# A selective-scan and expert-FFN kernel: the FFN's second layer one step later in TensorE's order

## Chip, cores and metric

One core of one Trainium2 chip. The metric is the time of one execution on the device, in microseconds (us). The kernel before took 3166.0 us (median of 3 runs, 3164.98 to 3170.4).

## What is computed

The input `x` has 32 rows (batch entries) of 512 tokens of 256 channels. Each row is normalised (`xn`), goes through a forward and a backward selective scan with 16 states each, and the sum is gated by an expert FFN. Cut to what matters:

```python
def _selective_scan(x, x_proj_w, dt_proj_w, dt_proj_b, A_log, Dp):
    A = -jnp.exp(A_log)
    dbc = jnp.einsum('bld,nd->bln', x, x_proj_w)
    delta, Bm, Cm = jnp.split(dbc, [DT_RANK, DT_RANK + D_STATE], axis=-1)
    delta = jax.nn.softplus(jnp.einsum('blr,dr->bld', delta, dt_proj_w) + dt_proj_b)
    deltaA = jnp.exp(delta[..., None] * A)
    BX = delta[..., None] * Bm[:, :, None, :] * x[..., None]
    ...
    y = jnp.einsum('blds,bls->bld', hs, Cm)
    return y + Dp * x

def _L0_ffn_ref(hidden_states, Wp1, bp1, Wp2, bp2, W1, b1, W2, b2, Wo, bo):
    ...
    h = jax.nn.gelu(jnp.einsum('bsh,bhf->bsf', hidden_states, w1) + b1[sel][:, None, :], approximate=False)
    reasoned = jnp.einsum('bsf,bfh->bsh', h, w2) + b2[sel][:, None, :]
    out = reasoned @ Wo + bo
    return hidden_states + 0.3 * out

xn = _layernorm(x, axis=-1)
s = scan_forward(xn) + scan_backward(xn)
g = _silu(_L0_ffn_ref(xn, ...))
x = x + s * g
```

The expert `sel` is picked once per row from its last token. The kernel multiplies W2 by Wo at the start, so that per row only two layers remain: `xn` by W1, then Gelu, then the product with W2·Wo.

## The kernel before, in words

The 32 rows are worked one after the other, each in 32 steps, one for each state (16 forward, 16 backward). All five engines have a program of their own, written out by hand; they meet by semaphores alone, and each engine works its own program strictly in its order. In step `s`:

- VectorE scans state `s` (`hs`, line 861) over 128 x 1024 values (two halves of the channels by 512 tokens), then multiplies the states of the step before by C (`hc`, line 840), for the states in `ON_DVE`. In step 1 it also forms the output `og` of the row before (line 833), and in step 0 the mean and variance of a later row (line 811).
- ScalarE makes the decay of state `s + 2` (line 692), scales `dxb` (line 595) for the states in `TURNED`, and copies what TensorE leaves in the one PSUM bank `front` (`fps`).
- GpSimd multiplies by B (`bx`, line 481) for the states that are not in `TURNED`, and by C (`hc`, line 469) for those in `POOL_C`, which are 2, 4, 5, 7, 9 and so on.
- TensorE broadcasts C of state `s + 1` into the PSUM bank `c` (line 1076), turns `dxb` of state `s + 3` into PSUM for the scan (line 1068), adds the skip term (line 1083) and the state products into `y` (line 1093). The broadcast waits until VectorE has used the last one.

While row `r` is scanned, the front of row `r + 1` (transposes, projections, step sizes, FFN) is worked in the same steps, in small pieces. The tables at lines 37 to 46 say in which step each piece is issued, separately for TensorE, ScalarE and GpSimd; numbers of 32 and more mean a step of the row's own scan (35 is its step 3). All pieces share the bank `front`, so each piece of TensorE waits until ScalarE has copied the one before.

The second FFN layer is issued by `ffn_out` (line 1024). It has eight parts, and two of them make one quarter, which is the gate's input for 128 tokens: four f32 products of `hT` with `w2o_sb` (line 1036), a bias product (line 1038) and the addition of `xn` (line 1039). Quarters 1 and 2 fill the bank, ScalarE's first gate copy (`gate_input`, line 637) moves it into `zz`, quarters 3 and 4 fill it again, and the second gate copy moves that. `FFN_OUT` lists the steps of the eight parts and `GATE` those of ScalarE's two copies; row 0 has tables of its own, `FFN_OUT_FIRST` and `GATE_FIRST`. The quarters wait for the Gelu (line 641), which ScalarE does at the end of step 31, between two loads of its function table. Later in ScalarE's order come the normalised row `xn` (line 558), its transposed copies (line 566) and the copy `projected` (line 575), for which VectorE's `low` (line 819) waits.

Within a step the order on TensorE is: broadcast, turn, skip term, adds, then the pieces of the front:

```python
if s + 1 in ON_DVE:
    broadcast_c(row, par, s + 1)
...
if s in ON_DVE:
    add_state(row, s)
front(row, par, s + STEPS, last)
if not last:
    front(row + 1, 1 - par, s)
```

Of the kernel before, what the change touches and what calls it, by code (L numbers as in the profile page):

```python
# [5 lines left out]
def mamba_moe_block(nc, x, xw_f, dtw_f, dtb_f, alog_f, d_f, xw_b, dtw_b, dtb_b, alog_b, d_b,  # L6
# [35 lines left out]
    LOG1P, STEPSIZE, DX, CUT = (26, 36), (27, 39), (28, 43), (29, 44)  # L42
    DX_TURN, DX_COPY = (28, 29, 44, 45), (30, 31, 46, 47)
    FFN_IN, HIDDEN, GELU = (16, 16, 18, 18, 20, 20, 22, 22), (18, 20, 22, 24), 31
    FFN_OUT, GATE = (31, 31, 32, 32, 34, 34, 35, 35), (35, 38)
    FFN_OUT_FIRST, GATE_FIRST = (33, 33, 34, 34, 36, 36, 37, 37), (36, 38)
    Y_OUT, Y_RESIDUAL = 1, 4
    SKIP = {0: ((0, 0), (2, 0)), 1: ((0, 1), (1, 0), (1, 1), (2, 1)), 4: ((3, 0), (3, 1))}
# [1196 lines left out]
```

## Time and profile before

| | |
|---|---|
| median of 3 runs | 3166.0 us |
| the profiled execution | 3168.72 us |
| its span in the profile | 3166.9 us |
| mean granted TensorE clock | 0.942 of full speed |
| busy: VectorE / ScalarE / GpSimd / TensorE | 96% / 94% / 93% / 82% |

The profile calls TensorE's matrix products PE and its weight loads PEld, VectorE DVE, ScalarE ACT, GpSimd POOL. Times are from the start of the span. In a timeline, consecutive like instructions are merged into one line with their count, and the bracket gives the idle time ahead of the line and what ended it; the end of a line overlaps the start of the next a little, since engines are pipelined. One row of the input takes some 96 us.

### The profile page before, as it was taken

How to read it: one execution, taken by the hardware profiler on the slowest of the kernel's cores; microseconds unless marked ns; L12 is line 12 of the kernel's file. 1: busy time of each engine (PE TensorE's matmuls, PEld its weight loads, DVE VectorE, ACT ScalarE, POOL GpSimd, SP SyncE). 2: the span in 40 equal slices, each digit the busy share in tenths (PEclk: the TensorE clock that was granted, in tenths of full speed). 3: DMA queues.
4: the chain of work that ended last, by engine and by line, in shares of the span. 5: the costliest groups of instructions: out<-in, count | busy, mean ns of one | idle time of the engine just before them, and what ended most of it. 6: DMA issues, size and time to landing. Idle time of an engine off the chain costs nothing. (4 is left out here: it accounts for less than half of the span.)

```text
span 3166.9 us, 49729 instructions
## 1 busy us (share of the span) xinstructions
PE 2591.2 (82%) x16278; PEld 2075.5 (66%) x16278; DVE 3027.4 (96%) x1964; ACT 2971.9 (94%) x5306; POOL 2945.8 (93%) x1454
## 2 busy tenths in 40 slices
PE   7888878888878888788888788887788887888886
PEld 5666666666667666666666666666666665666665
DVE  3999999999999999999999999999999999999998
ACT  5999999999999999999999999999999999999995
POOL 2899999999999999999999999999999999999996
PEclk9999999999999999999999999999999999999998
DMA  5443334443344443344433344433344333444331
GB/s 171 148 129 112 115 117 129 135 127 109 116 127 123 135 120 115 106 131 136 128 109 112 123 125 139 124 111 113 125 129 134 118 114 108 130 136 127 104 113 50
DMA packets 268759, 385.83 MB, mean 122 GB/s; under 512 B 44491, under 2 KB 118996, under 8 KB 268500
## 3 DMA queue, kind: packets, MB, share of 16 engines
q1 hardware_dynamic: 268500, 382.64, 39.8%
q8 instruction: 130, 2.13, 0.3%
q14 instruction: 129, 1.06, 0.1%
HBM read 340.59 MB, written 25.18 MB: 115 GB/s over the span
## 5 line engine op out<-in xcount | busy, mean ns | idle before, releaser
L481 POOL TENSOR_TENSOR bx<-dx,b_sb 128x1024 f32<-128x1024 f32 x576 | 1364.4, 2383 | 48.3 <-DVE hs L861 46.3
L861 DVE TENSOR_TENSOR_SCAN hs<-decay,bx 128x1024 f32<-128x1024 f32 x576 | 1306.6, 2278 | 11.3 <-ACT decay L692 6.4
L1093 PE MATMUL y<-ident,hc 128*128 128x128 f32 x8192 | 1097.9, 283 | 35.9 <-DVE hc L840 35.9
L469 POOL TENSOR_TENSOR hc<-hs,c_sb 128x1024 f32<-128x1024 f32 x448 | 1057.1, 2369 | 52.6 <-DVE hs L861 51.7
L1093 PEld LDWEIGHTS y<-ident,hc 128*128 128x128 f32 x8192 | 970.1, 146 | 144.3 <-DVE hc L840 99.9
L861 DVE TENSOR_TENSOR_SCAN hs<-decay_sb,decay 128x1024 f32<-128x1024 f32 x448 | 1009.8, 2271 | 39.5 <-PE decay L1068 24.3
L692 ACT ACTIVATE decay<-delta,rate 128x512 f32<-128x512 f32 x1152 | 745.6, 684 | 38.8 <-DVE hs L861 38.2
L595 ACT ACTIVATE dxb<-dxT,btok 128x256 f32<-128x256 f32 x1792 | 762.6, 504 | 0.6 <-PE decay L1068 0.6
L840 DVE TENSOR_TENSOR hc<-hs,c 128x1024 f32<-128x1024 f32 x576 | 690.8, 1199 | 28.9 <-PE c L1076 20.5
L1068 PE MATMUL decay<-ident,dxb 128*128 128x128 f32 x3584 | 482.1, 281 | 150.0 <-DVE hs L861 120.8
L1068 PEld LDWEIGHTS decay<-ident,dxb 128*128 128x128 f32 x3584 | 414.0, 144 | 289.7 <-issue 217.1
L692 ACT ACTIVATE decay_sb<-delta,rate 128x512 f32<-128x512 f32 x896 | 589.2, 716 | 0.0
L1076 PE MATMUL c<-dbc,selector 128*128 128x512 f32 x576 | 292.7, 508 | 290.8 <-DVE hc L840 290.8
L1076 PEld LDWEIGHTS c<-dbc,selector 128*128 128x128 f32 x576 | 113.1, 196 | 353.4 <-DVE hc L840 348.8
L1036 PE MATMUL front<-w2o_sb,hT 128*128 128x256 f32 x1024 | 296.2, 441 | 31.3 <-issue 31.3
L1020 PE MATMUL front<-xnT,w_sb 128*128 128x512 f32 x512 | 244.2, 599 | 41.9 <-ACT delta L608 41.9
L1036 PEld LDWEIGHTS front<-w2o_sb,hT 128*128 128x128 f32 x1024 | 217.8, 224 | 73.3 <-issue 41.7
L456 POOL TENSOR_TENSOR lg<-lg,ex 128x1024 f32<-128x1024 f32 x64 | 151.3, 2364 | 35.8 <-ACT lg L625 34.8
L1020 PEld LDWEIGHTS front<-xnT,w_sb 128*128 128x128 f32 x512 | 87.4, 190 | 116.7 <-issue 61.2
L461 POOL TENSOR_TENSOR delta<-lg,delta 128x1024 f32<-128x1024 f32 x64 | 152.5, 2382 | 0.1
L446 POOL TENSOR_TENSOR dx<-delta,xnT 128x1024 f32<-128x1024 f32 x64 | 152.5, 2382 | 0.1
L488 POOL TENSOR_TENSOR og<-og,xres 128x1024 f32<-128x1024 f32 x32 | 75.5, 2361 | 61.3 <-DVE og L833 61.3
(128 smaller groups left out, 2190.1 us busy)
## 6 DMA issues: line engine op xcount, KB each, us to landing
b_sb<-b_scratch SPq DMA_DIRECT2D x576, 256.0 KB, 3.3
c_sb<-b_scratch SPq DMA_DIRECT2D x448, 256.0 KB, 3.6
xin<-in_L_attn_x_dram SPq DMA_DIRECT2D x32, 512.0 KB, 7.7
w_sb<-in_L_ffn_W_dram SPq DMA_DIRECT2D x32, 512.0 KB, 3.4
w2o_sb<-w2o_scratch SPq DMA_DIRECT2D x32, 512.0 KB
xres<-in_L_attn_x_dram SPq DMA_DIRECT2D x32, 512.0 KB, 5.3
out_dram<-og SPq DMA_DIRECT2D x32, 512.0 KB, 4.4
dbc<-high SPq DMA_DIRECT2D x64, 128.0 KB, 2.4
```

Source lines behind the costliest of these rows:

```text
L446: nc.gpsimd.tensor_tensor(dx[:, g, :, :], delta[:, g * (1 + par), :, :], xnT[:, par, :, :], ALU.mult).then_inc(s_dx, 1)
L469: nc.gpsimd.tensor_tensor(hc[:, s % RING, :, :], hs[:, s % HSLOTS, :, :], c_sb[:, i % CRING, :].unsqueeze(1).broadcast_to([P, DT, T]), ALU ...
L481: nc.gpsimd.tensor_tensor(bx[:, i % RING, :, :], dx[:, g, :, :], b_sb[:, i % BRING, :].unsqueeze(1).broadcast_to([P, DT, T]), ALU.mult).th ...
L595: A(dxb[:, (row * NT + i) % XSLOTS, c, :], dxT[:, g, c, :], ACT.Copy, scale=btok[:, par, c, g, n:n + 1]).then_inc(s_dxb, 1)
L692: return A(to[:, k, :], delta[:, g * (1 + par), k, :], ACT.Exp, scale=rate[:, g, k, n:n + 1])
L840: V.tensor_tensor(hc[:, s % RING, :, :], hs[:, s % HSLOTS, :, :], cps[:, :].unsqueeze(1).broadcast_to([P, DT, T]), ALU.mult).then_inc(s_hc, 1)
L861: V.tensor_tensor_scan(hs[:, s % HSLOTS, :, :].rearrange("p k t -> p (k t)")[:, u], factor.rearrange("p k t -> p (k t)")[:, u], data.rearr ...
L1020: ins = M(fps[:, :], w1_sb[:, k, j * P:(j + 1) * P], xnT[:, par, k, :], start=(k == 0), stop=(k == DT - 1))
L1036: M(to, hT[:, j, c * P:(c + 1) * P], w2o_sb[:, j, :], start=(j == 0), stop=False)
L1068: ins = nc.tensor.transpose(dps[s % DSLOTS][:, k, c * P:(c + 1) * P], dxb[:, (row * NT + i) % XSLOTS, c, k * P:(k + 1) * P], ident[:, :])
L1076: M(cps[:, :], selector[:, N + n:N + n + 1].broadcast_to([P, P]), dbc[:, par, g, :], start=True, stop=True).then_inc(s_cps, 1)
L1093: ins = M(yps[:, c, k * P:(k + 1) * P], hc[:, s % RING, k, c * P:(c + 1) * P], ident[:, :], start=False, stop=(s == ADDED[-1]), is_transpo ...
```

## The change

The first two quarters are issued one step later each (31 and 32 become 32 and 33), the last two as well (34 and 35 become 35 and 36), and ScalarE's first gate copy moves from step 35 to 36. The second gate copy stays at 38, and row 0's own tables stay.

```diff
-    FFN_OUT, GATE = (31, 31, 32, 32, 34, 34, 35, 35), (35, 38)
+    FFN_OUT, GATE = (32, 32, 33, 33, 35, 35, 36, 36), (36, 38)
     FFN_OUT_FIRST, GATE_FIRST = (33, 33, 34, 34, 36, 36, 37, 37), (36, 38)
```

TensorE around the border of two rows, from the broadcast of C for state 0 to that for state 3. In `c<-dbc,selector`, `c` is the result and the rest the inputs. Before:

```order
L1076 MATMUL c<-dbc,selector 128x512
L1093 MATMUL y<-ident,hc 128x128 x8
L1036 MATMUL front<-w2o_sb,hT 128x256 x4
L1038 MATMUL front<-bias,ones 128x256
L1039 MATMUL front<-xn,ident 128x256
L1076 MATMUL c<-dbc,selector 128x512
L1083 MATMUL y<-dskip_diag,xnT 128x128 x2
L1093 MATMUL y<-ident,hc 128x128 x8
L1036 MATMUL front<-w2o_sb,hT 128x256 x4
L1038 MATMUL front<-bias,ones 128x256
L1039 MATMUL front<-xn,ident 128x256
L1083 MATMUL y<-dskip_diag,xnT 128x128 x4
```

With the change:

```order
L1093 MATMUL y<-ident,hc 128x128 x8
L1076 MATMUL c<-dbc,selector 128x512
L1083 MATMUL y<-dskip_diag,xnT 128x128 x2
L1093 MATMUL y<-ident,hc 128x128 x8
L1036 MATMUL front<-w2o_sb,hT 128x256 x4
L1038 MATMUL front<-bias,ones 128x256
L1039 MATMUL front<-xn,ident 128x256
L1083 MATMUL y<-dskip_diag,xnT 128x128 x4
L1093 MATMUL y<-ident,hc 128x128 x8
L1036 MATMUL front<-w2o_sb,hT 128x256 x4
L1038 MATMUL front<-bias,ones 128x256
L1039 MATMUL front<-xn,ident 128x256
```

The first quarter has moved from ahead of the broadcast for state 1 to behind the add of state 0; the second, from ahead of the skip term of step 1 to behind that step's add.

TensorE from the broadcast for state 3 to that for state 6. Before:

```order
L1076 MATMUL c<-dbc,selector 128x512
L1068 MATMUL decay<-ident,dxb 128x128 x8
L1036 MATMUL front<-w2o_sb,hT 128x256 x4
L1038 MATMUL front<-bias,ones 128x256
L1039 MATMUL front<-xn,ident 128x256
L1068 MATMUL decay<-ident,dxb 128x128 x8
L1093 MATMUL y<-ident,hc 128x128 x8
L1036 MATMUL front<-w2o_sb,hT 128x256 x4
L1038 MATMUL front<-bias,ones 128x256
L1039 MATMUL front<-xn,ident 128x256
L1083 MATMUL y<-dskip_diag,xnT 128x128 x2
L1093 MATMUL y<-ident,hc 128x128 x8
```

With the change:

```order
L1076 MATMUL c<-dbc,selector 128x512
L1068 MATMUL decay<-ident,dxb 128x128 x16
L1093 MATMUL y<-ident,hc 128x128 x8
L1036 MATMUL front<-w2o_sb,hT 128x256 x4
L1038 MATMUL front<-bias,ones 128x256
L1039 MATMUL front<-xn,ident 128x256
L1083 MATMUL y<-dskip_diag,xnT 128x128 x2
L1093 MATMUL y<-ident,hc 128x128 x8
L1036 MATMUL front<-w2o_sb,hT 128x256 x4
L1038 MATMUL front<-bias,ones 128x256
L1039 MATMUL front<-xn,ident 128x256
L1076 MATMUL c<-dbc,selector 128x512
```

The two turns for states 5 and 6 now stand side by side; the same instructions as before stand between the two broadcasts.

ScalarE at its first gate copy. Before:

```order
L692 ACTIVATE decay<-delta,rate 128x512 x2
L595 ACTIVATE dxb<-dxT,btok 128x256 x4
L637 ACTIVATE zz<-front 128x512
L595 ACTIVATE dxb<-dxT,btok 128x256 x4
L692 ACTIVATE decay_sb<-delta,rate 128x512 x2
```

With the change:

```order
L692 ACTIVATE decay<-delta,rate 128x512 x2
L595 ACTIVATE dxb<-dxT,btok 128x256 x8
L637 ACTIVATE zz<-front 128x512
L692 ACTIVATE decay_sb<-delta,rate 128x512 x2
L595 ACTIVATE dxb<-dxT,btok 128x256 x4
```

The copy `zz` stands one block of `dxb` later. VectorE's and GpSimd's orders do not change.

## Rows read from the trace of the kernel before

**Rows 1.** The page, busy us (share of the span) and instructions

```profile
PE 2591.2 (82%) x16278; PEld 2075.5 (66%) x16278; DVE 3027.4 (96%) x1964; ACT 2971.9 (94%) x5306; POOL 2945.8 (93%) x1454
```

**Rows 2.** The page's costliest groups: count | busy, mean ns | idle before, releaser

```profile
L861 DVE TENSOR_TENSOR_SCAN hs<-decay_sb,decay 128x1024 f32<-128x1024 f32 x448 | 1009.8, 2271 | 39.5 <-PE decay L1068 24.3
...
L840 DVE TENSOR_TENSOR hc<-hs,c 128x1024 f32<-128x1024 f32 x576 | 690.8, 1199 | 28.9 <-PE c L1076 20.5
```

**Rows 3.** Line 833's instructions: ns min/median/max, first and last start

```profile
L833 DVE TENSOR_TENSOR og<-y,zz x32: 1195/1199/1224, 179.7 to 3159.9; 128x1024 f32<-128x1024 f32 x32
```

**Rows 4.** VectorE's timeline at one row: start, us, engine, line [idle before]

```profile
1240.24 1.21 DVE L840 TENSOR_TENSOR hc<-hs,c 128x1024 f32<-128x1024 f32 x1
...
1243.57 1.20 DVE L840 TENSOR_TENSOR hc<-hs,c 128x1024 f32<-128x1024 f32 x1
...
1249.17 1.22 DVE L840 TENSOR_TENSOR hc<-hs,c 128x1024 f32<-128x1024 f32 x1
...
1253.43 2.29 DVE L861 TENSOR_TENSOR_SCAN hs<-decay_sb,decay 128x1024 f32<-128x1024 f32 x1 [0.84 <-PE decay L1068]
...
1258.48 1.22 DVE L840 TENSOR_TENSOR hc<-hs,c 128x1024 f32<-128x1024 f32 x1 [0.58 <-PE c L1076]
...
1271.66 0.67 DVE L819 TENSOR_TENSOR low<-front,high 128x512 fp32r<-128x512 f32 x1
```

**Rows 5.** TensorE's timeline at the same row

```profile
1235.25 0.79 PE L1076 MATMUL c<-dbc,selector 128*128 128x512 f32 x1 [1.94 <-DVE hc L840]
1235.84 1.91 PE L1093 MATMUL y<-ident,hc 128*128 128x128 f32 x8
1238.38 3.75 PE L1036 MATMUL front<-w2o_sb,hT 128*128 128x256 f32 x8 [0.63 <-issue]
...
1242.62 0.58 PE L1076 MATMUL c<-dbc,selector 128*128 128x512 f32 x1
...
1244.35 1.89 PE L1036 MATMUL front<-w2o_sb,hT 128*128 128x256 f32 x8
...
1246.92 1.05 PE L1083 MATMUL y<-dskip_diag,xnT 128*128 128x128 f32 x8
...
1248.60 0.48 PE L1076 MATMUL c<-dbc,selector 128*128 128x512 f32 x1
...
1257.91 0.48 PE L1076 MATMUL c<-dbc,selector 128*128 128x512 f32 x1
```

**Rows 6.** Windows: length, PE, PEld, DVE, ACT, POOL busy, granted clock, DMA

```profile
1242.00:1258.00 16.00, 16.00 (x104) 13.64 (x103) 15.03 (x8) 15.32 (x37) 14.67 (x11) 1.00 0.31 99
1235.20:1242.00 6.80, 6.12 (x17) 4.45 (x17) 6.66 (x12) 6.76 (x7) 5.30 (x3) 0.50 0.37 131
```

**Rows 7.** ScalarE's timeline at the same row

```profile
1247.28 0.58 ACT L637 ACTIVATE zz<-front 128x512 f32<-128x512 f32 x1
1247.76 1.70 ACT L595 ACTIVATE dxb<-dxT,btok 128x256 f32<-128x256 f32 x4
...
1256.88 0.60 ACT L637 ACTIVATE zz<-front 128x512 f32<-128x512 f32 x1 [0.55 <-PE front L1039]
1257.57 2.08 ACT L558 ACTIVATE xn<-xin,shift,rs 128x256 f32<-128x256 f32 x4
1259.55 1.32 ACT L692 ACTIVATE decay_sb<-delta,rate 128x512 f32<-128x512 f32 x2
...
1270.80 0.58 ACT L575 ACTIVATE projected<-front 128x512 f32<-128x512 f32 x1
```

**Rows 8.** TensorE's timeline: the start of work at another stretch of low clock

```profile
1504.23 0.50 PE L1076 MATMUL c<-dbc,selector 128*128 128x512 f32 x1 [2.81 <-DVE hc L840]
```

**Rows 9.** Windows of these two stretches, columns as in rows 6

```profile
1504.80:1508.20 3.40, 3.40 (x18) 3.30 (x17) 3.40 (x3) 2.95 (x5) 3.34 (x3) 0.51 0.00 0
...
1526.08:1532.10 6.02, 6.02 (x15) 4.33 (x16) 5.55 (x5) 5.98 (x14) 3.56 (x3) 0.50 0.19 66
```

**Rows 10.** Grouped lines: line 637

```profile
L637 ACT ACTIVATE zz<-front 128x512 f32<-128x512 f32 x64 | 37.9, 592 | 26.8 <-PE front L1039 26.5
```

## The prediction

> **What bounds the kernel now.** The page's busy shares come first [rows 1]. VectorE is busy 96% of the span, GpSimd 93%, ScalarE 94%, TensorE 82%. VectorE runs the scans; a time can change only by changing how long VectorE is idle. Outside the head of the program its idle time is small: the costliest groups [rows 2] put 39.5 us before the scans of turned states and 28.9 us before its `hc` products, 68.4 us together. So little can a change of order give back, while nothing caps a loss.
>
> The period of a row comes from the `og` products, of which there are 32, the first at 179.7 and the last at 3159.9 us [rows 3]: 2980.2 / 31 = 96.14 us. I read one row in detail, the one whose `og` starts at 1239.13 (the next one comes 96.09 us later by the same count of work, close to the mean).
>
> VectorE's timeline there [rows 4] has two waits, both on TensorE: 0.84 us before scan 6, and 0.58 us before the product of state 6, which needs that state's C broadcast. TensorE's timeline [rows 5] says why. It waits 0.63 us for the Gelu, then runs from 1238.38 without a gap. The windows [rows 6] confirm it: busy 16.00 of 16.00 us from 1242.00 to 1258.00. So **TensorE, idle on average, is the late engine in the first seven steps of a row**, and the four quarters of the second FFN layer stand inside that stretch. It is a queue worked in order: what is put into it delays all behind it.
>
> **The change, part by part.** I call the quarters F01, F23, F45, F67, the broadcasts c0, c1, c3, c6 by their state, and T5, T6 the turns of b*x.
>
> Nothing is added or removed. F01 leaves the end of step 31, where it stood between c0's add and c1, and goes behind c1, the skip term and the add of state 0. The others move down likewise; F67 still stands ahead of c6. The move is made for rows 1 to 31, 31 times. No DMA and no GpSimd instruction moves, and SyncE's waits for these units are due at its step 10, long after.
>
> 1. *The place that F01 leaves.* TensorE's last add before it starts at 1235.84 and takes 1.91, to 1237.75. Now the next instruction is c1, which waits for VectorE's product of state 0: 1240.24 + 1.21 = 1241.45, so it starts at about 1241.5. Before, c1 started at 1242.62. It is **1.12 us earlier**, but VectorE has no use for it: its product of state 1 comes at 1243.57 and did not wait [rows 4, 5]. TensorE idles 3.75 us instead of 0.63. The wait for the Gelu disappears, for F01 could start by 1238.38 as before.
>
> 2. *The place where F01 arrives.* At full clock a quarter takes 1246.92 - 1244.35 = **2.57 us** [rows 5]. From c1 to c3 stood c1, skip, add, F23, skip, add: 1248.60 - 1242.62 = 5.98 us, of which all now stays, plus F01. So c3 starts at 1241.5 + 5.98 + 2.57 = 1250.05, not 1248.60, if the clock is full.
>
> 3. *The clock.* TensorE ran at 1.2 GHz (granted 0.50) from 1235.2 to 1242.0 and at 2.4 GHz behind that [rows 6]. The low stretch began after 1.94 us without work, and ended after 3.6 us of unbroken work (1238.38 to 1242.0). At the row of 1526 it ended after 6.0 us of unbroken work (1526.08 to 1532.1), at 1504 after 4.0 (1504.23 to 1508.2) [rows 8, 9]. Now there is more idle time in the low stretch, and work begins at 1241.5; no row has that long a pause there. The bounds: nothing (the clock rises at 1242.0 anyway), and 6.0 us at half speed, 3.0 us lost. I take 4 us, as two of the three cases have, so **2.0 us lost**. That puts c3 at 1252.05.
>
> The Trainium skill, "TensorE: Matmul & The Clock Gate", Part 1, says that for modeling the ramp penalty is under 1% of a typical kernel span. By that rule this term would be at most 31.7 us in all, against my 31 x 2.0 = 62 us; the trace already has low stretches in every row looked at, so I keep the rows' figure.
>
> 4. *From c3 to c6.* The same instructions as before, in another order: 1257.91 - 1248.60 = 9.31 us. They ran without a gap before, so c6 starts at 1252.05 + 9.31 = 1261.36. That is 2.57 - 1.12 + 2.0 = **3.45 us later** per row. Inside it the shares differ. VectorE waits for c3 about 3.4 us (product 3 starts near 1252.6 instead of 1249.17). T6 now follows T5 directly, so the 0.84 us before scan 6 goes. At product 6 it waits again, some 1.6 us. Sum 5.0 against 1.42 before. F45 waits for ScalarE's first gate copy, which comes right behind F23 and takes 0.58 us [rows 7]; T5, T6 and an add (3 x 0.87 us) cover that, so it costs nothing.
>
> 5. *ScalarE behind it.* Its first gate copy stands one block of `dxb` later (4 copies, 1.70 us with the overlap), which alone is free. But it then waits for F23, until 1252.1; it would be there at 1248.9. The second copy waits for F67, until 1261.4, where it ran at 1256.88. ScalarE is thus 4.5 us late when VectorE is 3.45 late, about 1.1 us more. Behind the copy stand `xn` (2.0 us) and the decay of state 9 (1.3): 1261.4 + 0.7 + 2.0 + 1.3 = 1265.4. Scan 9 follows product 6 (1258.48, 1.2 us) and scan 8 (2.3 us [rows 2]), so it started near 1262.0 and would now at 1265.4, with nothing in hand. The late copy is also ahead of the copy `projected`, which ended at 1271.38, 0.28 us before VectorE's `low` [rows 7, 4]. So ScalarE's lag costs between 0 (it catches up, being idle 6% of the span [rows 1]) and 1.1 us; I take **0.8**, since 1.1 - 0.28 is what the second of these places shows.
>
> *The sum:* 3.45 + 0.8 = 4.25 us a row, times 31 = 131.8 us. The profiled execution took 3168.7 us (span 3166.9); 3168.7 + 131.8 = 3300.5. It stands 2.7 above the median of 3166.0, so the forecast is **3298 us**, 4.2% slower.
>
> **The rivals.** A measurement of this kernel can tell about 0.2%, 6 us, from no change.
>
> *The clock rises with the work* (term 3 near nothing, as the skill's rule would have it nearer than mine). Then c6 is 2.57 - 1.12 = 1.45 us late and ScalarE adds 0 to 0.8: 45 to 70 us, 3211 to 3236. For it: the rise at 1242.0 came in spite of a pause. Against: before that rise TensorE had worked, and now it has not.
>
> *The low clock lasts 6 us of work.* Term 3 is 3.0 and ScalarE's lag costs its 1.1: (1.45 + 3.0 + 1.1) x 31 = 172, so 3338. The row at 1526 speaks for it; others for less.
>
> *Faster: TensorE catches up.* T6 and c6 come in time, since F45 no longer stands between T5 and T6, and their waits of 0.84 us or more vanish: 31 x 0.84 = 26 us, 3140. It needs c3 out by 1249.17 - 0.55 = 1248.6, which leaves 7.1 us from 1241.5 for work that takes 5.98 + 2.57 = 8.55 at full clock. Only quarters under 1.1 us each would decide so; the rows have 2.57.
>
> *No change:* VectorE has 1.4 us of waits there that could absorb as much. But c6 itself is among the late ones, so there is no slack behind it; and the order shows that the move is made.
>
> **How the numbers follow.** Forecast 0.74, clock rises at once 0.10, long low clock 0.11, faster 0.03, no change 0.02. The range reaches from the upper part of the first rival, 3225, to the end of the second, 3338. Faster 0.03, within 0.2% 0.02, slower 0.95.
>
> **What would show it.** VectorE's wait before product 1 stays near nothing, one of 2.5 to 4 us appears before product 3, the one before scan 6 goes, and the one before product 6 grows to 1 to 2 us. TensorE shows a pause of 3 to 4 us ahead of c1 in each row, `<- DVE hc`, and the low stretch there is longer than 6.8 us. ScalarE's idle time before line 637, 26.8 us now [rows 10], passes 100 us. If the idle time before scans of line 861 grows by more than that of line 840, I am wrong about the place; if low stretches are not longer, about term 3.

## The result, and the profile after

The changed kernel takes 3301.3 us (median of 4 runs, 3300.4 to 3301.7) against 3165.5 us before: a ratio of 1.0426, with a 95% interval of 1.0408 to 1.0444. It is slower by 136 us. The profiled execution has a span of 3299.3 us.

The first rows to read are the same groups as in [rows 2], and line 637 as in [rows 10]:

```profile
L861 DVE TENSOR_TENSOR_SCAN hs<-decay,bx 128x1024 f32<-128x1024 f32 x576 | 1308.2, 2281 | 12.7 <-ACT decay L692 6.4
...
L861 DVE TENSOR_TENSOR_SCAN hs<-decay_sb,decay 128x1024 f32<-128x1024 f32 x448 | 1009.7, 2271 | 34.3 <-ACT decay_sb L692 17.7
L840 DVE TENSOR_TENSOR hc<-hs,c 128x1024 f32<-128x1024 f32 x576 | 690.9, 1199 | 149.0 <-issue 103.8
...
L637 ACT ACTIVATE zz<-front 128x512 f32<-128x512 f32 x64 | 38.5, 601 | 163.4 <-PE front L1039 163.4
```

The work of VectorE's groups is unchanged to 0.2%. Its idle time before its `hc` products grew by 120.1 us (28.9 to 149.0), while that before the turned scans fell by 5.2 and its releaser changed from TensorE's turns to ScalarE's decays. ScalarE waits six times as long for the quarters (26.8 to 163.4).

The period of a row, from line 833 as in [rows 3]:

```profile
L833 DVE TENSOR_TENSOR og<-y,zz x32: 1196/1201/1226, 178.6 to 3292.2; 128x1024 f32<-128x1024 f32 x32
```

(3292.2 - 178.6) / 31 = 100.44 us, 4.30 us more than the 96.14 before; 31 x 4.30 = 133 us, nearly all of the loss. One row in VectorE's timeline, from its `og` on, the places of [rows 4], and with them three waits that the kernel before had smaller or not at all:

```profile
1185.49 1.20 DVE L833 TENSOR_TENSOR og<-y,zz 128x1024 f32<-128x1024 f32 x1
...
1199.48 1.22 DVE L840 TENSOR_TENSOR hc<-hs,c 128x1024 f32<-128x1024 f32 x1 [3.97 <-issue]
...
1208.78 1.22 DVE L840 TENSOR_TENSOR hc<-hs,c 128x1024 f32<-128x1024 f32 x1 [1.39 <-PE c L1076]
...
1212.58 2.29 DVE L861 TENSOR_TENSOR_SCAN hs<-decay_sb,decay 128x1024 f32<-128x1024 f32 x1 [0.38 <-issue]
...
1222.92 0.69 DVE L819 TENSOR_TENSOR low<-front,high 128x512 fp32r<-128x512 f32 x1 [0.25 <-ACT projected L575]
1224.20 2.29 DVE L861 TENSOR_TENSOR_SCAN hs<-decay_sb,decay 128x1024 f32<-128x1024 f32 x1 [0.59 <-ACT decay_sb L692]
```

These are the products of states 3 and 6, scan 9, and the low part with the scan behind it. The wait before scan 6 is gone. In the kernel before, the scan behind the low part was this:

```profile
1272.70 4.46 DVE L861 TENSOR_TENSOR_SCAN hs<-decay_sb,decay 128x1024 f32<-128x1024 f32 x2 [0.36 <-issue]
```

From start to start the row divides into three stretches. From `og` to product 3 it takes 13.99 us, against 1249.17 - 1239.13 = 10.04 in the row of [rows 4]. From product 3 to product 6 it takes 9.30, against 9.31. From product 6 to the scan behind the low part it takes 15.42, against 14.22. So 1.20 us are lost behind product 6, more than the 0.86 by which the waits in brackets grew there (0.38 + 0.25 + 0.59 - 0.36): the rest stands in no bracket. Three instructions of this stretch that used to start some 0.1 us before the end of the one ahead no longer do. TensorE's timeline, with the C broadcasts for states 0, 1, 3 and 6 as in [rows 5]:

```profile
1181.61 0.50 PE L1076 MATMUL c<-dbc,selector 128*128 128x512 f32 x1 [1.94 <-DVE hc L840]
...
1187.87 0.80 PE L1076 MATMUL c<-dbc,selector 128*128 128x512 f32 x1 [4.88 <-DVE hc L840]
...
1191.02 2.96 PE L1036 MATMUL front<-w2o_sb,hT 128*128 128x256 f32 x8
...
1198.80 0.58 PE L1076 MATMUL c<-dbc,selector 128*128 128x512 f32 x1
...
1208.11 0.58 PE L1076 MATMUL c<-dbc,selector 128*128 128x512 f32 x1
```

From c1 to c3 it takes 10.93 us, from c3 to c6 9.31, the latter to the digit what it took before. At full clock the first stretch would take 5.98 + 2.57 = 8.55 by the rows of before, so low clock cost this row 2.38 us. In the next row the two broadcasts stand at 1289.13 and 1298.93, 9.80 apart, and it cost 1.25. The windows of both rows, columns as in [rows 6]:

```profile
1183.00:1193.20 10.20, 5.33 (x19) 4.79 (x20) 10.18 (x10) 10.14 (x20) 7.46 (x6) 0.50 0.18 55
1193.20:1208.00 14.80, 14.80 (x92) 12.26 (x91) 10.20 (x6) 9.59 (x21) 12.28 (x8) 1.00 0.33 107
1285.40:1292.20 6.80, 3.07 (x13) 2.98 (x14) 6.80 (x5) 6.74 (x16) 4.33 (x3) 0.50 0.21 74
```

The granted clock is at its lower level (1.2 GHz) for 10.2 us in one row and 6.8 us in the other, and rows of the two kinds follow each other almost to the end, 101.3 and 100.1 us long. ScalarE's two gate copies and what stands behind, as in [rows 7]:

```profile
1199.19 0.60 ACT L637 ACTIVATE zz<-front 128x512 f32<-128x512 f32 x1 [3.86 <-PE front L1039]
...
1208.49 0.60 ACT L637 ACTIVATE zz<-front 128x512 f32<-128x512 f32 x1 [1.84 <-PE front L1039]
1209.19 2.08 ACT L558 ACTIVATE xn<-xin,shift,rs 128x256 f32<-128x256 f32 x4
1211.17 1.32 ACT L692 ACTIVATE decay_sb<-delta,rate 128x512 f32<-128x512 f32 x2
```

The decay of state 9 ends at 1212.49, and scan 9 starts at 1212.58, having waited 0.38.

### The profile page after: what moved, and what is told of

Its sections match the earlier page's. It is cut to its first block and busy times, and to the rows that moved or that the text cites. A ratio compares the mean times of both kernels' runs of the same rounds, so it can differ in the third digit from the quotient of the medians.

```text
span 3299.3 us, 49729 instructions
## 1 busy us (share of the span) xinstructions
PE 2581.2 (78%) x16278; PEld 2092.4 (63%) x16278; DVE 3037.4 (92%) x1964; ACT 2970.1 (90%) x5306; POOL 2951.4 (89%) x1454
## 5 line engine op out<-in xcount | busy, mean ns | idle before, releaser
L1093 PEld LDWEIGHTS y<-ident,hc 128*128 128x128 f32 x8192 | 987.4, 147 | 139.7 <-DVE hc L840 94.5
L840 DVE TENSOR_TENSOR hc<-hs,c 128x1024 f32<-128x1024 f32 x576 | 690.9, 1199 | 149.0 <-issue 103.8
L1076 PE MATMUL c<-dbc,selector 128*128 128x512 f32 x576 | 301.2, 523 | 438.0 <-DVE hc L840 438.0
L1068 PE MATMUL decay<-ident,dxb 128*128 128x128 f32 x3584 | 497.9, 288 | 147.3 <-DVE hs L861 140.4
L1068 PEld LDWEIGHTS decay<-ident,dxb 128*128 128x128 f32 x3584 | 432.9, 149 | 280.3 <-issue 211.8
L1036 PE MATMUL front<-w2o_sb,hT 128*128 128x256 f32 x1024 | 258.4, 398 | 0.0
L1036 PEld LDWEIGHTS front<-w2o_sb,hT 128*128 128x128 f32 x1024 | 198.4, 204 | 24.6
L637 ACT ACTIVATE zz<-front 128x512 f32<-128x512 f32 x64 | 38.5, 601 | 163.4 <-PE front L1039 163.4
```

Of the source, the lines that this page charges most:

```text
L840: V.tensor_tensor(hc[:, s % RING, :, :], hs[:, s % HSLOTS, :, :], cps[:, :].unsqueeze(1).broadcast_to([P, DT, T]), ALU.mult).then_inc(s_hc, 1)
L1036: M(to, hT[:, j, c * P:(c + 1) * P], w2o_sb[:, j, :], start=(j == 0), stop=False)
L1068: ins = nc.tensor.transpose(dps[s % DSLOTS][:, k, c * P:(c + 1) * P], dxb[:, (row * NT + i) % XSLOTS, c, k * P:(k + 1) * P], ident[:, :])
L1076: M(cps[:, :], selector[:, N + n:N + n + 1].broadcast_to([P, P]), dbc[:, par, g, :], start=True, stop=True).then_inc(s_cps, 1)
L1093: ins = M(yps[:, c, k * P:(k + 1) * P], hc[:, s % RING, k, c * P:(c + 1) * P], ident[:, :], start=False, stop=(s == ADDED[-1]), is_transpo ...
```

## The experiments

Eleven kernels ran. All edits are against the changed kernel unless said otherwise; each time is set against the kernel before, run on the same chip.

### Which part of the move: TensorE's or ScalarE's

```diff
-    FFN_OUT, GATE = (32, 32, 33, 33, 35, 35, 36, 36), (36, 38)
+    FFN_OUT, GATE = (32, 32, 33, 33, 35, 35, 36, 36), (35, 38)
```

> TensorE's four quarters stand one step later as in the change, ScalarE's first gate copy stays at step 35. Theory (TensorE's order is the cause, the copy waits for the second quarter wherever it stands): 3295 to 3305 us, the same as the whole change. Rival (the copy's later place costs its block of dxb, 1.6 us a row): 31 x 1.6 = 50 us less, about 3250.

Measured: 3303.6 us, ratio 1.0437 (1.0419 to 1.0454). The whole loss is there without ScalarE's edit, but not by the same waits. With the copy one block of `dxb` earlier, product 6 does not wait; the scan ahead of it waits instead, for ScalarE's decay:

```profile
1203.91 2.29 DVE L861 TENSOR_TENSOR_SCAN hs<-decay,bx 128x1024 f32<-128x1024 f32 x1 [1.63 <-issue]
```

From product 3 to the scan behind the low part it takes 24.72 us in both kernels (1196.69 to 1221.41 here, 1199.48 to 1224.20 in the change). The second half alone, on the tables of before:

```diff
-    FFN_OUT, GATE = (31, 31, 32, 32, 34, 34, 35, 35), (35, 38)
+    FFN_OUT, GATE = (31, 31, 32, 32, 34, 34, 35, 35), (36, 38)
```

> The quarters stand as before, only ScalarE's first gate copy is one step later. Theory: the third quarter starts at 1249.79 in the row read, the copy would end at about 1249.5, so only rows with a longer low clock pay: 0 to 0.6 us a row, 3166 to 3184 us. Rival (the copy's place is worth 1.6 us a row): about 3215.

Measured: 3169.5 us, ratio 1.0015 (1.0006 to 1.0025). The later place of the copy costs 4 to 5 us by itself, and nothing where the copy waits for its quarter anyway.

### Which quarter

```diff
-    FFN_OUT, GATE = (32, 32, 33, 33, 35, 35, 36, 36), (36, 38)
+    FFN_OUT, GATE = (32, 32, 32, 32, 34, 34, 35, 35), (35, 38)
```

> Only the first quarter moves, from the end of step 31 to the end of step 0, directly ahead of the second. Theory: it carries the 3.45 us a row (place and clock), but the second quarter now ends 1.8 us sooner than with the whole change and the fourth 1.2 us sooner, so ScalarE is hardly late: 3166 + 107 = 3273, between 3250 and 3285. Rival (the loss is all TensorE's late C broadcasts and needs no ScalarE): 3301, as the whole change.

Measured: 3250.3 us, ratio 1.0263 (1.0246 to 1.0281), 84 us over the kernel before and at the lower edge of what was expected. VectorE's waits in one row:

```profile
1181.14 1.22 DVE L840 TENSOR_TENSOR hc<-hs,c 128x1024 f32<-128x1024 f32 x1 [2.93 <-issue]
...
1185.40 2.29 DVE L861 TENSOR_TENSOR_SCAN hs<-decay_sb,decay 128x1024 f32<-128x1024 f32 x1 [0.84 <-PE decay L1068]
...
1190.45 1.22 DVE L840 TENSOR_TENSOR hc<-hs,c 128x1024 f32<-128x1024 f32 x1 [0.58 <-PE c L1076]
...
1204.66 4.47 DVE L861 TENSOR_TENSOR_SCAN hs<-decay_sb,decay 128x1024 f32<-128x1024 f32 x2 [0.36 <-issue]
```

The three later waits are those of the kernel before, to the digit. One new wait, 2.93 us at product 3, is all that was added. Scan 9 and the low part do not wait for ScalarE: the second and fourth quarter end early enough here.

The complement:

```diff
-    FFN_OUT, GATE = (32, 32, 33, 33, 35, 35, 36, 36), (36, 38)
+    FFN_OUT, GATE = (31, 31, 33, 33, 35, 35, 36, 36), (36, 38)
```

> The first quarter stays in step 31; quarters two to four and the gate copy move as in the change. Theory: the broadcasts for states 3 and 6 keep their place behind the same work, but the quarters end 1.8 and 1.2 us later for ScalarE, which passes part of it on: 0.5 to 1.2 us a row, 3180 to 3203. Rival (only the first quarter matters): 3166, within 6.

Measured: 3211.7 us, ratio 1.0143 (1.0126 to 1.0160), 46 us over, a little above what was expected. VectorE's waits in one row:

```profile
1175.22 1.22 DVE L840 TENSOR_TENSOR hc<-hs,c 128x1024 f32<-128x1024 f32 x1 [1.27 <-PE c L1076]
...
1179.01 2.29 DVE L861 TENSOR_TENSOR_SCAN hs<-decay_sb,decay 128x1024 f32<-128x1024 f32 x1 [0.37 <-issue]
...
1189.33 0.69 DVE L819 TENSOR_TENSOR low<-front,high 128x512 fp32r<-128x512 f32 x1 [0.25 <-ACT projected L575]
1190.62 4.46 DVE L861 TENSOR_TENSOR_SCAN hs<-decay_sb,decay 128x1024 f32<-128x1024 f32 x2 [0.59 <-ACT decay_sb L692]
```

Here the product of state 6 waits 1.27 us instead of 0.58 after 0.84, so TensorE's part is the same as before; what is new are ScalarE's three waits, with 0.37 + 0.25 + (0.59 - 0.36) = 0.85 us in brackets, and 1175.22 to 1190.62, 15.40 us from start to start, as in the whole change (before: 14.22). The row shown takes 97.1 us, 1.0 more than the row of [rows 4]. It is the shortest of three kinds; the others take 98.0 and 98.4. In them TensorE's clock is still low when c1 is issued (to 1063.0, with c1 at 1061.5), and products 1 and 3 wait up to 0.47 and 0.59 us. The two halves of the move together make 84 + 46 = 130 us of the 136.

### The clock

The changed kernel, with transposes of the identity into the bank `front` in the pause that the first quarter left. They read nothing that the kernel makes, and the first quarter overwrites them.

```diff
+            def keep_busy(row, n):
+
+                pe.wait_ge(s_dxT, row * 4 + 2)
+                for i in range(n):
+                    nc.tensor.transpose(fps[:, i % C * P:(i % C + 1) * P], ident[:, :], ident[:, :])
...
                     if s in ON_DVE:
                         add_state(row, s)
+                    if s + 1 == STEPS and not last:
+                        keep_busy(row + 1, 28)
                     front(row, par, s + STEPS, last)
```

> The changed kernel with 28 more transposes of the identity into the free bank front in the pause that the first quarter left (their result is overwritten by the first quarter; 28 x 0.11 = 3.1 us of work at full clock in a pause of 3.7). Theory (term 3: low clock behind the pause costs about 2.0 us a row): 31 x 2.0 = 62 us less, 3225 to 3250. Rival (the order alone makes the loss, the clock nothing): 3301. If the filler itself delays the broadcast for state 1, above 3301.

Measured: 3243.4 us, ratio 1.0248 (1.0231 to 1.0265): 58 us less than the change, 1.9 a row. VectorE's waits in one row, and TensorE's filler, C broadcast for state 3 and clock:

```profile
1166.23 1.20 DVE L833 TENSOR_TENSOR og<-y,zz 128x1024 f32<-128x1024 f32 x1
...
1177.65 1.22 DVE L840 TENSOR_TENSOR hc<-hs,c 128x1024 f32<-128x1024 f32 x1 [1.41 <-issue]
...
1186.96 1.22 DVE L840 TENSOR_TENSOR hc<-hs,c 128x1024 f32<-128x1024 f32 x1 [1.38 <-PE c L1076]
...
1190.75 2.29 DVE L861 TENSOR_TENSOR_SCAN hs<-decay_sb,decay 128x1024 f32<-128x1024 f32 x1 [0.38 <-issue]
```

```profile
1164.03 4.41 PE L1204 MATMUL front<-ident 128*128 128x128 f32 x28
1168.61 0.50 PE L1076 MATMUL c<-dbc,selector 128*128 128x512 f32 x1 [0.16 <-DVE hc L840]
...
1176.98 0.58 PE L1076 MATMUL c<-dbc,selector 128*128 128x512 f32 x1
```

```profile
1162.00:1166.20 4.20, 3.85 (x20) 3.78 (x21) 4.05 (x10) 4.15 (x4) 4.03 (x2) 0.63 0.58 163
1166.20:1180.00 13.80, 13.64 (x95) 11.95 (x94) 12.39 (x9) 12.47 (x30) 11.19 (x9) 0.99 0.27 81
```

The low clock now falls on the filler and is over before c1 is issued. The wait at product 3 is 1.41 instead of 2.85 or 3.97; the others stay as they were. The clock is thus worth 1.44 to 2.56 us in a row, 2.0 in the mean. From c1 to c3 it takes 8.37 us at full clock, a little less than the 8.55 worked out above. Product 3 starts 11.42 us after `og`, 1.38 later than in the row of [rows 4]: that is what the place costs there, clock apart. Not every row is mended: in the row where c1 stands at 478 most of the filler ran at the lower clock and took 5.13 us, c1 came 0.9 us late, and product 3 waited 2.31.

### Are the late C broadcasts the cause, or only where it shows

```diff
-                    if s + 1 in ON_DVE:
+                    if s + 1 in ON_DVE and s + 1 not in EARLY_C:
                         broadcast_c(row, par, s + 1)
...
                     if s in ON_DVE:
                         add_state(row, s)
+                        for n in EARLY_C:
+                            if on_dve(n) == on_dve(s) + 1:
+                                broadcast_c(row, par, n)
```

with `EARLY_C = (3, 6)`.

> The changed kernel, but TensorE broadcasts C for states 3 and 6 right behind the add of states 1 and 3, ahead of the second and the fourth quarter, so that VectorE's products 3 and 6 need not wait for them. By step 4 of the prediction taken literally (the lateness of the broadcasts is the loss): the waits of 2.9 to 4.0 and 1.4 us a row go, down to 3301 - 31 x 4.8 = 3152. Rival (all of TensorE's unbroken work is late, the turns for states 5, 8 and 9 and ScalarE's gate copies with it, and the broadcast is only where it shows): the waits move to scans 5 and 9, 3290 to 3310 us.

Measured: 3317.6 us, ratio 1.0479 (1.0462 to 1.0497), 16 us more than the change and above both expectations. The waits of one row:

```profile
1201.68 1.22 DVE L840 TENSOR_TENSOR hc<-hs,c 128x1024 f32<-128x1024 f32 x1 [1.50 <-issue]
1205.06 4.46 DVE L861 TENSOR_TENSOR_SCAN hs<-decay_sb,decay 128x1024 f32<-128x1024 f32 x2 [2.16 <-PE decay L1068]
1210.11 2.29 DVE L861 TENSOR_TENSOR_SCAN hs<-decay,bx 128x1024 f32<-128x1024 f32 x1 [0.58 <-issue]
...
1214.37 2.29 DVE L861 TENSOR_TENSOR_SCAN hs<-decay_sb,decay 128x1024 f32<-128x1024 f32 x1 [0.86 <-PE decay L1068]
1217.58 2.29 DVE L861 TENSOR_TENSOR_SCAN hs<-decay_sb,decay 128x1024 f32<-128x1024 f32 x1 [0.92 <-ACT decay_sb L692]
```

Product 6 does not wait any more, product 3 waits less, and the sum is not smaller: scans 5 and 8 wait for TensorE's turns in its place, and scan 9 for ScalarE longer than before (0.92 against 0.38), since the broadcasts now stand ahead of the quarters. From product 3 to the scan behind the low part it takes 1201.68 to 1229.20, 27.52 us, against 24.72 in the change. In other rows product 3 waits only 0.24 or 0.67, and they take 101.5 and 100.7 us, little less than the 101.6 of the one shown; in the first of them a low clock further on in the row makes a scan wait 1.11 us for its turn, so part of the 16 us is the clock's. The broadcast is where the lateness shows. The cause is the length of TensorE's unbroken work from c1 on, whatever stands first in it.

### ScalarE's share

The decay of state 9 is made at the start of ScalarE's step 6, ahead of the second gate copy, instead of behind it and `xn`.

```diff
-    AHEAD, AHEAD_NEXT = {5: 8, 14: 22, 15: 24, 16: 26, 23: 28, 26: 29, 27: 30}, {29: 5}
+    AHEAD, AHEAD_NEXT = {5: 8, 6: 9, 14: 22, 15: 24, 16: 26, 23: 28, 26: 29, 27: 30}, {29: 5}
```

> The changed kernel, with ScalarE's decay of state 9 made at the start of step 6, ahead of the second gate copy, in whose wait it fits (1.2 us). Theory (term 5: ScalarE is late behind the gate copies): VectorE's wait of 0.37 us before scan 9 goes, and the ones at the low part (0.25 + 0.23 us more) shrink as ScalarE uses its idle time: 3262 to 3290 us. Rival (ScalarE's lag is hidden): 3301.

Measured: 3250.0 us, ratio 1.0265 (1.0248 to 1.0282): 51 us less than the change, more than expected. The profiled execution is the slowest of its four (3257.6). In its row at 1188 the waits are 2.92 at product 3, 1.39 at product 6 and 0.59 at the scan behind the low part; those before scan 9 and before the low part are gone. ScalarE at the second gate copy:

```profile
1195.13 1.32 ACT L692 ACTIVATE decay_sb<-delta,rate 128x512 f32<-128x512 f32 x2
1197.07 0.60 ACT L637 ACTIVATE zz<-front 128x512 f32<-128x512 f32 x1 [0.62 <-PE front L1039]
```

The decay fits in the wait, which shrank from 1.84 to 0.62 us. The direct gain is the 1.20 us between product 6 and the scan behind the low part (most rows are back at 14.2), 37 us in all. The other 14 us came from elsewhere: the wait at product 3 falls from 4.29 us in the first row to 3.0 in the fifth and is 2.8 to 2.9 in most behind, where the change has 2.85 and 3.97 in turn. A row of 98.9 us instead of 100.4 meets the low clock in another way. That is read from the trace and was not tested by itself.

### Both mends at once

The changed kernel with the filler of 28 and the earlier decay:

```diff
-    AHEAD, AHEAD_NEXT = {5: 8, 14: 22, 15: 24, 16: 26, 23: 28, 26: 29, 27: 30}, {29: 5}
+    AHEAD, AHEAD_NEXT = {5: 8, 6: 9, 14: 22, 15: 24, 16: 26, 23: 28, 26: 29, 27: 30}, {29: 5}
...
                     if s in ON_DVE:
                         add_state(row, s)
+                    if s + 1 == STEPS and not last:
+                        keep_busy(row + 1, 28)
```

> The changed kernel with both mends: 28 filler transposes and the decay of state 9 ahead of the gate copy. If the loss is place + clock + ScalarE, the two mends add up: 3301 - 58 - 51 = 3192, and what is left over 3165 is the place, 31 x (2.57 - 1.12) = 45 us at most: 3185 to 3212. Rival (the two mends cure the same wait): about 3240.

Measured: 3214.5 us, ratio 1.0156 (1.0141 to 1.0172), 2.5 us above the range expected, and 87 us less than the change instead of 109. What the second mend had won through the clock cannot be won twice; without it the sum is 58 + 37 = 95, and 8 us stay open. One row, and line 833, from the fastest of the four runs (3208.2):

```profile
1358.94 1.22 DVE L840 TENSOR_TENSOR hc<-hs,c 128x1024 f32<-128x1024 f32 x1 [1.41 <-issue]
...
1368.25 1.22 DVE L840 TENSOR_TENSOR hc<-hs,c 128x1024 f32<-128x1024 f32 x1 [1.39 <-PE c L1076]
```

```profile
L833 DVE TENSOR_TENSOR og<-y,zz x32: 1194/1199/1225, 174.1 to 3199.3; 128x1024 f32<-128x1024 f32 x32
```

Its period is (3199.3 - 174.1) / 31 = 97.59 us, 1.45 over the 96.14 of before. That this is just 2.57 - 1.12 is partly chance. Two rows in three take 97.5 us, but the others up to 98.7, and the 96.14 of before has low clock in it as well. What the place costs with the clock out of both kernels is read below.

### The same filler in the kernel before

Nothing but the filler, 14 transposes ahead of the broadcast for state 0, on the tables of before.

```diff
                 for s in range(STEPS):
+                    if s + 1 == STEPS and not last:
+                        keep_busy(row + 1, 14)
                     if s + 1 in ON_DVE:
```

> The kernel before, with 14 transposes of the identity into the free bank front (overwritten by the first quarter) in the pause ahead of the broadcast for state 0. Theory: no low clock at the first quarter, which then takes 2.6 us and not 4.2; VectorE's waits before scan 6 and product 6 (1.42 us a row) shrink: 20 to 50 us less, 3120 to 3146. Rival (the Gelu's end and ScalarE set the pace of these steps anyway): 3160 to 3168.

Measured: 3143.2 us, ratio 0.9930 (0.9914 to 0.9947), 22 us faster than the kernel before. Its rows alternate between 95.3 and 95.8 us. In the second kind the clock still falls while TensorE waits 1.75 us for the Gelu, so a filler was put there as well:

```diff
                     if s in ON_DVE:
                         add_state(row, s)
+                    if s + 1 == STEPS and not last:
+                        keep_busy(row + 1, 12)
```

> The kernel before with fillers in both pauses: 14 transposes ahead of the broadcast for state 0 and 12 ahead of the first quarter (1.3 us in the wait for the Gelu, 1.75 us long in the run with one filler). Theory: the low clock that came in every second row with one filler (its rows were 95.82 and 95.31 us) goes, so all rows take 95.3: 31 x 0.26 = 8 us less than 3143, 3130 to 3139. Rival (the first quarter starts at the Gelu's end, and VectorE's last waits are ScalarE's): 3140 to 3146.

Measured: 3141.4 us, ratio 0.9928 (0.9914 to 0.9941): 2 us less than with one, no difference that could be told, and short of what was expected. It lies in the rival's range. Most rows now take 95.3 us, the first nine without exception, but behind them every fourth or fifth takes 96.5: a low clock appears in another place of the row:

```profile
1106.90:1113.70 6.80, 5.64 (x23) 5.16 (x24) 6.61 (x4) 5.22 (x10) 6.74 (x5) 0.52 0.05 17
```

```profile
1114.55 2.29 DVE L861 TENSOR_TENSOR_SCAN hs<-decay_sb,decay 128x1024 f32<-128x1024 f32 x1 [1.04 <-PE decay L1068]
```

TensorE waits 2.82 us for VectorE there, then works at half speed, and a scan waits 1.04 us for a turn. With ScalarE's decay of state 9 moved ahead as well, by the same edit of `AHEAD` as above (`6: 9` added):

> As the last one, and ScalarE's decay of state 9 ahead of the second gate copy. Theory: in the kernel before ScalarE hardly waits at that copy and VectorE's only ScalarE waits are small (0.15 to 0.2 us a row), so 0 to 6 us less than the one without. Rival (ScalarE's order is worth as much as in the changed kernel, 1.6 us a row): 50 us less, about 3085.

Measured: 3139.5 us, ratio 0.9917 (0.9903 to 0.9930). It is the fastest of all, 0.8% below the kernel before; the interval against the last two overlaps. The rival, 50 us for ScalarE's order, is out: without late quarters there is nothing for it to cure.

This kernel and the changed one with both mends differ in the place of the quarters and the gate copy, and in where the fillers stand. Undisturbed rows take 95.3 us here and 97.5 there, so the place costs 2.2 us a row when the clock is out of both. The 1.4 us above is less because the kernel before paid for the clock already: its first quarter ran at 1.2 GHz and took 3.75 us for the products that take 1.89 at full clock [rows 5].

## Why the prediction was right

The forecast was 3298 us, the median is 3301.3. Point by point:

- *What bounds the kernel.* Right. TensorE has the least busy time of the four engines and still is the late one in the first steps of a row.
- *Term 1, c1 earlier and of no use.* Right for the row read, and there is no wait before product 1 in the changed kernel. In every fifth row of the kernel before c1 came later, as at 1530.75, and products 1 and 3 waited 0.47 and 0.54 us; there the earlier c1 is of use. The pause was longer than the 3.75 us of the row read, 4.88, since the add ahead of it ran at full clock.
- *Term 2, the place.* 2.57 - 1.12 = 1.45 us a row; with the clock mended, product 3 comes 1.38 us later.
- *Term 3, the clock.* Taken as 2.0 us. By c1 to c3 it is 2.38 and 1.25 in the two kinds of rows, a mean of 1.8, by the wait at product 3 it is 2.56 and 1.44, a mean of 2.0, and the filler won 1.9. One sign came only by half: the low stretch was to be longer than 6.8 us, and it is so in one row of two (10.2), while in the other it is 6.8 again. The Trainium skill ("TensorE: Matmul & The Clock Gate", Part 1) says that for modeling the ramp penalty is under 1% of a typical kernel span. The estimate by it was 31.7 us at most; the filler won 58 us, 1.8% of the span, so the rows were the better guide.
- *Term 4, from c3 to c6.* 9.31 us forecast and measured. The first wait was put at 3.4 us (mean measured 3.41), the second at 1.6 (1.39), and the wait before scan 6 went. What failed here is a reading, not the size: the step spoke of the late broadcasts as if they were the loss. The run with early broadcasts has less of these waits and is slower still.
- *Term 5, ScalarE.* This is the one term that was mis-sized: taken as 0.8 us, between 0 and 1.1, and measured as 1.20. The two places were named rightly, but ScalarE, with 6% of idle time, did not catch up before them. Putting the decay ahead won 51 us, 37 of them this term and the rest through the clock of the rows. So the terms do not quite add up: the clock's share depends on the length of a row.
- *The sum.* 4.25 us a row against 4.30 measured by line 833. So close a match is partly luck. The pair of rows read makes 1.38 + 2.0 + 1.20 = 4.6 over the row of [rows 4]. Over the first 29 rows it is 4.47, (3099.19 - 178.57) / 29 against (2970.67 - 179.65) / 29, because some rows of before were longer than the one read; and the last two rows, which the change lengthens by 1.9 us each, bring it to 4.30.
- *The rivals.* That the clock rises with the work, and that it stays low for 6 us of work, both fail as rules for all rows. After c1 at 1187.87 the clock rose at 1193.2, after c1 at 1289.13 at 1292.2: 5.3 and 3.1 us of work, a mean of 4.2 where 4 was taken. Faster and no change are out by the interval.

## What to carry to other kernels

- An engine with 18% of idle time can be the bound of a stretch. Look for its longest run without a gap, and for what is queued behind; what is moved out of a pause into that run costs its full length, less only what the work ahead of it gains.
- The pause that is left costs again where TensorE's clock falls in it. Here the place cost 1.4 us a row, the clock 2.0 and ScalarE's lag 1.2, and some transposes of nothing in the pause of the kernel before made it 0.7% faster.
- Measure a loss from start to start of the same two instructions, before and after. The waits in brackets showed 0.86 us where 1.20 were lost.
- When a wait names its releaser, test whether it is the cause. Take the releaser earlier and see whether the time goes or the wait moves.

## What was not expected of the hardware

- Rows of a strictly periodic program are not alike. In the changed kernel rows with 10.2 us and with 6.8 us at the lower clock alternate, with 101.3 and 100.1 us between their `og` products. The kernel before has a pattern of five rows, from 95.8 to 97.2 us. When the length of a row changes, so does the pattern, and a mend wins more or less than its own part (51 us for 37).
- Work in a pause does not have to be at full clock to help: the 28 filler transposes took 4.41 us in the row shown, since the clock was low for part of them, against 3.22 in a row at full clock (275), and c1 was not late. Where it took 5.13 us, since most of it ran at the lower clock, c1 was late.
